# Scan layer on one core: the last time block's sum over half of the states moved from VectorE to GpSimd, and a new order around it

## The chip, the core and the metric

The kernel runs on 1 core of one Trainium2 chip, in float32. The metric is the device time of one execution in microseconds (us). Engines are named as the profile does: PE is TensorE, PEld its weight loads, DVE VectorE, ACT ScalarE, POOL GpSimd, SP SyncE.

## The reference

Two sequences (B = 2) of 1024 steps and 256 features pass a row filter, a selective state-space layer with 16 states over 512 channels, and then a much smaller attention and feed-forward part whose result is one row per sequence. The changed work is in the state-space layer:

```python
xi = jax.nn.silu(conv(xi) + conv_b)          # 4 taps over time, per channel
dt, Bm, Cm = split(xi @ x_proj)
delta = jax.nn.softplus(dt @ dt_w + dt_b)
def step(h, inputs):
    d_t, x_t, B_t, C_t = inputs
    dA = jnp.exp(d_t[..., None] * A)
    h = dA * h + (d_t * x_t)[..., None] * B_t[:, None, :]
    y = jnp.einsum('bds,bs->bd', h, C_t)     # sum over the 16 states
    return (h, y)
y = (y + xi * D) * jax.nn.silu(z)
return x + y @ out_proj
```

## The kernel before

The 2 x 1024 steps are cut into four chunks of T = 512 steps (`NCH` = 4, two per sequence, `c` = 0 to 3). In a chunk the 16 states (`NS`, `s`) are worked one after another; `n = 16 * c + s` counts them over the whole loop, 0 to 63. The 512 channels are 4 tiles `m` of 128 partitions, and the 512 steps are 4 time blocks `i` of 128. For one state the work goes round the engines:

- GpSimd, `input_step(n, pair)`: delta * x * B for two tiles at a time into a slot of the ring `hb` of `RING` = 4 states (L1353). It may run four states ahead; a slot is free once the transposes of state n - 4 are done.
- ScalarE, `exp_step(n, m)`: the decay `dA` of one tile into one of two PSUM halves (L1217); the half is free once the scan two tiles back is done.
- VectorE, `scan_step(n, m)`: the scan over 512 steps of a tile (L1686).
- TensorE, `transposes(n, i)`: time block `i` of all four tiles, turned so that time lies on the partitions, into PSUM half `hT[i % 2]` (L794). Blocks 0 and 2 use half 0, blocks 1 and 3 half 1, and a half must have been read before it is written again.
- Blocks 0 and 2 are multiplied by C by ScalarE, `mul_step` (L1227, into `hc`), and summed over the states in PSUM by TensorE, `reduce`. Blocks 1 and 3 are multiplied and summed by VectorE in one instruction, `mac_step`, called the sum step here (L1702, into `yTd`).

The loops of the engines run one state behind each other: in the iteration of state n, VectorE scans state n and then sums state n - 1, and ScalarE and TensorE work on the transposes of n - 1. An iteration has two halves, h = 2n and 2n + 1: tiles 0, 1 with block 1's sum, and tiles 2, 3 with block 3's sum.

Beside this run jobs: what the next chunk needs (prologue) and what the last chunk leaves (epilogue). Their order is written by hand, as tables from half-iteration to jobs. T: transposed input; I: input projection of a tile; V: four convolution taps of a tile by TensorE (3 tiles; tile 1, `POOL_TILE`, is convolved by GpSimd in `conv_taps`, L1386 to L1391); X: projection to dt, B and C; XT: C transposed; D: delta of a tile; Z: gate of a tile; Y: the sums of blocks 1 and 3 turned back; O: output projection. TensorE makes a job in its half, after that half's transposes; ScalarE and VectorE read it one half later:

```python
def to_read(h):
    return BESIDE[h - 1] if h else []
```

V is read by ScalarE (half of it as a copy, then a tanh, L1024 and L1025) and then by VectorE (L1483). D is read by ScalarE (absolute value L1066, then exponential and logarithm L1086 and L1088, with a load of the function table before the first) and then by VectorE (L1497). Jobs alternate between two PSUM banks, so a job waits until the one two places back is read. GpSimd also makes a diagonal scaling for each chunk (`row_scaling`, L1372) and the products of delta and x for the next chunk (`step_times_input`, L1403).

## Time and profile before

| | us |
|---|---|
| three runs | 580.72, 580.25, 576.88 |
| median | 580.25 |
| profiled execution | 581.45 |
| its span from first to last instruction | 579.3 |
| busy PE, PEld | 481.0, 339.3 |
| busy DVE, ACT, POOL | 485.7, 352.5, 357.9 |
| scan loop, first scan to last | 43.6 to 512.3 |

All busy times and rows are of the one profiled execution. The scan loop is the part from 43.6 to 512.3 us; before it lies the head for the first chunk, after it the attention and feed-forward rows. An engine's busy time in the whole says little here, since the four chunks differ in what they carry.

### The profile page before, as it was taken

What the parts mean: (1) busy time and instruction counts of PE and PEld (TensorE: products, weight loads), DVE (VectorE), ACT (ScalarE), POOL (GpSimd) and SP (SyncE); (2) the same over time, 40 slices, a digit from 0 to 9 for tenths busy, and PEclk for the clock granted to TensorE, in tenths of its full rate; (3) what the DMA queues carried; (4) which work ended last, traced back from release to release, by engine and by line L of the source; (5) the groups of instructions that cost most, each with busy time, mean ns of one, the idle gap of its engine ahead of it and who ended that gap; (6) DMA issues with size and microseconds to landing.
All of it is one profiled execution on the core that took longest, in us unless ns stands there. A gap on an engine that the chain in (4) does not pass through costs nothing.

```text
span 579.3 us, 7844 instructions
## 1 busy us (share of the span) xinstructions
PE 481.0 (83%) x2753; PEld 339.3 (59%) x2753; DVE 485.7 (84%) x569; ACT 352.5 (61%) x612; POOL 357.9 (62%) x215
## 2 busy tenths in 40 slices
PE   8968998789668999796689998966897867889992
PEld 6424664465457666554566665545785555878651
DVE  4779989987999899989998999799999989861512
ACT  3765666678765667886757768877466557521210
POOL 5039699747884698777856987787567548100001
PEclk9979999857999999979999999799998879699997
DMA  9331011110111011111110110111111860019004
GB/s 292 101 112 36 37 37 37 39 38 36 37 36 37 36 39 40 36 37 37 38 36 26 48 40 37 37 37 36 38 37 37 294 259 1 1 47 369 13 1 150
DMA packets 17918, 38.87 MB, mean 67 GB/s; under 512 B 1665, under 2 KB 10497, under 8 KB 17874
## 3 DMA queue, kind: packets, MB, share of 16 engines
q1 hardware_dynamic: 17874, 38.32, 19.0%
q8 instruction: 24, 0.39, 0.3%
q14 instruction: 20, 0.16, 0.1%
HBM read 36.08 MB, written 2.23 MB: 66 GB/s over the span
## 4 chain that ended last, share of the span: by engine, by line
PE 36%; DVE 33%; issue 16%; ACT 7%; POOL 6%; DVEq 0%; POOLq 0%; ACTq 0%
DVE scanmem L1686 19%; DVE yTd L1702 8%; PE hT L794 6%; PE pp L508 5%; POOL scanmem L1353 5%; PE pp L532 4%; PE pp L592 3%; PE yacc L566 3%; PE dA L765 2%; PE pp L558 2%; ACT hc L1227 2%; DVE yTd L1611 1%; PE pp L736 1%; PE yacc L562 1%; PE pp L664 1%
## 5 line engine op out<-in xcount | busy, mean ns | idle before, releaser
L1353 POOL TENSOR_TENSOR scanmem<-par,scanmem 128x1024 f32<-128x1024 f32 x128 | 299.1, 2362 | 94.7 <-PE hT L794 59.8
L1217 ACT ACTIVATE dA<-par,Aneg 128x512 f32<-128x512 f32 x256 | 172.5, 690 | 71.3 <-DVE scanmem L1686 70.2
L794 PE MATMUL hT<-con,scanmem 128*128 128x128 f32 x1024 | 158.7, 293 | 60.5 <-DVE yTd L1702 36.8
L794 PEld LDWEIGHTS hT<-con,scanmem 128*128 128x128 f32 x1024 | 122.0, 149 | 118.7 <-DVE yTd L1702 49.0
L1686 DVE TENSOR_TENSOR_SCAN scanmem<-dA,carry,scanmem 128x512 f32<-128x512 f32 x128 | 156.9, 1269 | 2.5 <-ACT dA L1217 2.4
L1686 DVE TENSOR_TENSOR_SCAN scanmem<-dA,scanmem 128x512 f32<-128x512 f32 x128 | 149.2, 1208 | 3.4 <-ACT dA L1217 3.0
L1227 ACT ACTIVATE hc<-hT,CTs 128x512 f32<-128x512 f32 x128 | 87.2, 681 | 78.1 <-PE hT L794 77.6
L1702 DVE SCALAR_TENSOR_TENSOR yTd<-hT,CTs,yTd 128x512 f32<-128x512 f32 x120 | 87.9, 733 | 10.9 <-PE hT L794 10.7
L566 PE MATMUL yacc<-con,hc 128*128 128x128 f32 x512 | 77.1, 293 | 5.8 <-ACT hc L1227 5.8
L566 PEld LDWEIGHTS yacc<-con,hc 128*128 128x128 f32 x512 | 63.2, 151 | 10.0 <-ACT hc L1227 6.5
L508 PE MATMUL pp<-xnT,wi 128*128 128x512 f32 x120 | 63.1, 658 | 5.1 <-ACT xnT L993 3.2
L532 PE MATMUL pp<-xr,diag 128*128 128x512 f32 x88 | 39.4, 592 | 0.0
L508 PEld LDWEIGHTS pp<-xnT,wi 128*128 128x128 f32 x120 | 23.1, 212 | 25.4 <-issue 18.6
L1423 POOL TENSOR_TENSOR par<-xt,hc 128x1024 f32<-128x1024 f32 x1 | 2.4, 2352 | 52.8 <-ACT hc L1269 52.8
L592 PE MATMUL pp<-wo,par 128*128 128x256 f32 x128 | 28.9, 380 | 0.8 <-DVE par L1467 0.8
L592 PEld LDWEIGHTS pp<-wo,par 128*128 128x128 f32 x128 | 23.8, 191 | 4.0 <-DVE par L1467 1.1
L532 PEld LDWEIGHTS pp<-xr,diag 128*128 128x128 f32 x88 | 16.0, 190 | 16.8 <-issue 16.5
L558 PE MATMUL pp<-dbc,wdt 17*128 17x512 f32 x28 | 19.8, 807 | 2.8 <-DVE par L1497 2.8
L1497 DVE SCALAR_TENSOR_TENSOR par<-pp,par 128x512 f32<-128x512 f32 x14 | 9.6, 690 | 13.2 <-ACT par L1088 10.5
L765 PE MATMUL dA<-con 128*128 128x128 f32 x110 | 17.1, 289 | 0.0
L765 PEld LDWEIGHTS dA<-con 128*128 128x128 f32 x110 | 13.9, 192 | 4.7 <-issue 4.6
L1386 POOL TENSOR_SCALAR par<-xr,half_w,half_b 128x512 f32<-128x512 f32 x3 | 2.3, 762 | 23.0 <-ACT xr L1013 23.0
(194 smaller groups left out, 487.8 us busy)
## 6 DMA issues: line engine op xcount, KB each, us to landing
scanmem<-brow SPq DMA_DIRECT2D x32, 512.0 KB, 3.6
par<-in SPq DMA_DIRECT2D x1, 4096.0 KB, 18.1
scanmem<-in SPq DMA_DIRECT2D x1, 4096.0 KB, 15.1
xt<-in SPq DMA_DIRECT2D x4, 512.0 KB, 6.5
wi<-in SPq DMA_DIRECT2D x2, 1024.0 KB, 6.7
out<-par SPq DMA_DIRECT2D x4, 512.0 KB, 4.1
aw<-in SPq DMA_DIRECT2D x5, 256.0 KB, 6.6
xr<-in SPq DMA_DIRECT2D x1, 1024.0 KB, 8.8
```

The source lines that it names most:

```text
L508: last = mm(o, win[:, k, col:col + P], xnT[:, k, :], start=k == 0, stop=k == KD - 1)
L532: last = mm(o, dg[:, m, k, :], xr3[:, m, k:k + T], start=k == 0, stop=k == KC - 1)
L558: return mm(o, wdt[:, m * P:(m + 1) * P], dbc[0:DR + 1, :], start=True, stop=True)
L566: return mm(o[:, m * P:(m + 1) * P], src, ident, start=False, stop=last, is_transpose=True, skip_group_check=True)
L592: last = mm(o[:, i * DM:(i + 1) * DM], dx(e)[:, m, t0:t0 + P], wo[:, m, :], start=m == 0, stop=m == CT - 1)
L765: mm(dst, ident, ident, start=True, stop=True)
L794: last = nc.tensor.transpose(hT[:, i % 2, m * P:(m + 1) * P], hb[:, n % RING, m, i * P:(i + 1) * P], ident)
L1217: A(dA[:, m % 2, :], delta(c)[:, m, :], ACT.Exp, scale=Aneg[:, m * NS + s:m * NS + s + 1]).then_inc(da_ready, 1)
L1227: A(hc[:, e % 2, :], hT[:, 0, :], ACT.Copy, scale=CTs[:, c % 2, i, s:s + 1]).then_inc(mul_done, 1)
L1353: nc.gpsimd.tensor_tensor(hb[:, n % RING, ms, :], dx(c)[:, ms, :], Bb[:, row:row + 1, :].to_broadcast([P, 2, T]), ALU.mult).then_inc(bx_re ...
L1686: V.tensor_tensor_scan(hb[:, n % RING, m, :], dA[:, m % 2, :], hb[:, n % RING, m, :], start, ALU.mult, ALU.add).then_inc(scan_done, 1)
L1702: V.scalar_tensor_tensor(dst, src, cs, dst, ALU.mult, ALU.add).then_inc(mac_done, 1)
```

## The change

The sum over the states for block 3 of 38 of the 64 states is split: ScalarE multiplies the transposed block by C into SBUF (`pool_mul_step`) and GpSimd adds it to `yTd` (`add_step`). These are the odd states of chunks 0 to 2 and states 1 to 14 of chunk 3 (`by_pool`). In GpSimd's program the addition for state n - 4 stands between the two `input_step`s of state n. TensorE's transposes of block 1 of state n wait for ScalarE's product where state n - 1 is such a state. Then the order:

- ScalarE makes `exp_step(n + 1, 0)` ahead of the second part of the reading of a job (V's tanh, D's softplus), and that part in the first half behind `exp_step(n, 2)`.
- VectorE reads V and D (`LATE`) one half later than before, behind the half's first scan.
- I of tile 1 is made first, and GpSimd's taps lie at states 5, 6 and 7 where they were at 4 and 5; its finishing of the tile at 9 (7 before), the step times input at 14 and 15 (13 and 14 before).
- X moves from slot 14 to 15, O of the second half from 16 to 17, D and Z to one slot each, up to 26.

```diff
@@ -50,21 +50,23 @@
-PROLOGUE = {3: [("T", 0), ("T", 1)], 4: [("I", 0)], 5: [("I", 1)], 6: [("I", 2)], 7: [("I", 3)], 8: [("V", 0)],
-            10: [("V", 2)], 12: [("V", 3)], 14: [("X", 0)], 18: [("XT", 0), ("D", 0)], 20: [("D", 1), ("D", 2)], 21: [("D", 3)],
-            22: [("Z", 0)], 23: [("Z", 1)], 24: [("Z", 2)], 25: [("Z", 3)]}
-EPILOGUE = {1: [("Y", 1), ("Y", 3)], 11: [("O", 0)], 16: [("O", 1)], 28: [("R", 0)], 30: [("R", 1)]}
+PROLOGUE = {3: [("T", 0), ("T", 1)], 4: [("I", 1)], 5: [("I", 0)], 6: [("I", 2)], 7: [("I", 3)], 8: [("V", 0)],
+            10: [("V", 2)], 12: [("V", 3)], 15: [("X", 0)], 18: [("XT", 0), ("D", 0)], 20: [("D", 1)], 21: [("D", 2)], 22: [("D", 3)],
+            23: [("Z", 0)], 24: [("Z", 1)], 25: [("Z", 2)], 26: [("Z", 3)]}
+EPILOGUE = {1: [("Y", 1), ("Y", 3)], 11: [("O", 0)], 17: [("O", 1)], 28: [("R", 0)], 30: [("R", 1)]}
 LAST_EPILOGUE = {1: [("Y", 1)], 2: [("Y", 3)], 3: [("O", 0)], 5: [("O", 1)], 17: [("R", 0)], 19: [("R", 1)]}
 ATT = [6, 8, 8, 10, 12, 14, 15, 16, 17, 20, 22, 23, 24, 27]
 ATT1 = [28, 29]
 HEAD_CONV = 2
 EARLY_I = [2, 3, 0, 1]
 POOL_TILE = 1
-POOL_AT = [4, 5]
+FIRST_I = POOL_TILE
+POOL_AT = {5: range(0, 2), 6: range(2, 3), 7: range(3, KC)}
 SCALING_AT = 3
-DX_AT = [13, 14]
-POOL_TANH_AT = 11
-POOL_FINISH_AT = 7
+DX_AT = [14, 15]
+POOL_TANH_AT = 12
+POOL_FINISH_AT = 9
+LATE = ("V", "D")
 def product_convs(n):
...
@@ -141,9 +143,35 @@
 INDEX = {job: q for q, job in enumerate(ORDER)}
+def by_pool(n):
+
+    c, s = n // NS, n % NS
+    return 0 < s < NS - 1 if c == NCH - 1 else s % 2 == 1
+
+
+def pool_sums(n):
+
+    return sum(by_pool(j) for j in range(n + 1))
+
+
+def vector_sums(n, i):
+
+    return 2 * n + (i + 1) // 2 - pool_sums(n if i == 3 else n - 1)
+
+
 def to_read(h):
     return BESIDE[h - 1] if h else []
+
+
+def read_by_vector(h):
+
+    return [job for job in to_read(h) if job[0] not in LATE]
+
+
+def read_late(h):
+
+    return [job for job in to_read(h - 1) if job[0] in LATE] if h else []
...
@@ -248,6 +276,10 @@
         def gate(n):
             return par[n % 2][:, 3, :].rearrange("p (m t) -> p m t", m=CT)
+        def for_pool(n):
+            room = xnT if n // NS == NCH - 1 else sm[:, :].rearrange("p (a t) -> p a t", t=T)
+            return room[:, pool_sums(n) % 2, :]
+
         def scaling(n):
             return par[n % 2][:, 1, 0:NT * P].rearrange("p (i t) -> p i t", i=NT)
...
@@ -568,7 +601,10 @@
             def job_Y(job, o):
                 _, e, i = job
-                pe.wait_ge(mac_done, 2 * (NS * (e + 1) - 1) + i // 2 + 1)
+                n = NS * (e + 1) - 1
+                pe.wait_ge(mac_done, vector_sums(n, i))
+                if i == 3 and by_pool(n):
+                    pe.wait_ge(pool_sum_done, pool_sums(n))
                 if e < NCH - 1:
                     for m in range(CT):
                         skip(o, e, i, m, m == 0)
...
@@ -787,9 +823,15 @@
                 if i == 0:
                     pe.wait_ge(scan_done, CT * (n + 1))
                 e = 2 * n + i // 2
-                if e >= 1:
-
-                    pe.wait_ge(mac_done if i % 2 else mul_done, e)
+                if i % 2 == 0 and e >= 1:
+                    pe.wait_ge(mul_done, e)
+                if i == 3:
+                    pe.wait_ge(mac_done, vector_sums(n, 1))
+                if i == 1 and n:
+                    if by_pool(n - 1):
+                        pe.wait_ge(pool_mul_done, pool_sums(n - 1))
+                    else:
+                        pe.wait_ge(mac_done, vector_sums(n - 1, 3))
                 for m in range(CT):
                     last = nc.tensor.transpose(hT[:, i % 2, m * P:(m + 1) * P], hb[:, n % RING, m, i * P:(i + 1) * P], ident)
                 last.then_inc(hT_ready, 1)
...
@@ -1022,8 +1064,11 @@
                     act.wait_ge(half_ready, 1)
                 A(xi(n)[:, m, :], o, ACT.Identity, bias=half_b[:, m:m + 1], scale=0.5)
+                return None
+
+            def product_tanh(job, o):
+                m = job[2]
                 A(o, o, ACT.Tanh, bias=half_b[:, m:m + 1], scale=0.5).then_inc(product_tanh_ready, 1)
-                return None
             def ev_X(job, o):
...
@@ -1142,8 +1187,8 @@
                     exp_ln_table()
                 if name == "D":
                     softplus(n, i)
-                if name == "S1":
-                    softmax(n)
+                if name == "V":
+                    product_tanh(job, bank(job))
             def read(job):
                 if job[0] in evs:
...
@@ -1226,6 +1274,15 @@
                     act.wait_ge(red_done, e - 1)
                 A(hc[:, e % 2, :], hT[:, 0, :], ACT.Copy, scale=CTs[:, c % 2, i, s:s + 1]).then_inc(mul_done, 1)
+            def pool_mul_step(n):
+
+                c, s = n // NS, n % NS
+                if by_pool(n):
+                    act.wait_ge(hT_ready, NT * n + 4)
+                    if pool_sums(n) > 2:
+                        act.wait_ge(pool_sum_done, pool_sums(n) - 2)
+                    A(for_pool(n), hT[:, 1, :], ACT.Copy, scale=CTs[:, c % 2, 3, s:s + 1]).then_inc(pool_mul_done, 1)
+
             def carry_step(n):
                 c, s = n // NS, n % NS
                 if c % HALVES == 0:
...
@@ -1235,21 +1292,30 @@
             for c in range(NCH):
                 for s in range(NS):
                     n = c * NS + s
-                    exp_step(n, 0)
+                    if n == 0:
+                        exp_step(n, 0)
                     exp_step(n, 1)
                     if n:
                         mul_step(n - 1, 0)
                     for job in to_read(2 * n):
                         read(job)
+                    exp_step(n, 2)
+                    for job in to_read(2 * n):
+                        after_job(job)
                     if c + 1 < NCH and 2 * s == POOL_TANH_AT:
                         pool_conv_tanh(c + 1)
-                    exp_step(n, 2)
                     exp_step(n, 3)
                     if n:
                         mul_step(n - 1, 2)
-                        carry_step(n - 1)
                     for job in to_read(2 * n + 1):
                         read(job)
+                    if n + 1 < NCH * NS:
+                        exp_step(n + 1, 0)
+                    for job in to_read(2 * n + 1):
+                        after_job(job)
+                    if n:
+                        pool_mul_step(n - 1)
+                        carry_step(n - 1)
                     if c + 1 < NCH and 2 * s + 1 == POOL_TANH_AT:
                         pool_conv_tanh(c + 1)
             n = NCH * NS
...
@@ -1354,6 +1420,18 @@
             own = Own(pool, pool_own)
+            def add_step(n):
+
+                c = n // NS
+                if by_pool(n):
+                    if by_pool(n - 1):
+                        pool.wait_ge(pool_sum_done, pool_sums(n - 1))
+                    else:
+                        pool.wait_ge(mac_done, vector_sums(n - 1, 3))
+                    pool.wait_ge(pool_mul_done, pool_sums(n))
+                    dst = yTd[:, c % 2, 1, :]
+                    nc.gpsimd.tensor_tensor(dst, dst, for_pool(n), ALU.add).then_inc(pool_sum_done, 1)
+
             def conv_finish(n):
                 acc, t = xi(n)[:, POOL_TILE, :], delta(n)[:, POOL_TILE, :]
...
@@ -1408,14 +1486,18 @@
                     if c + 1 < NCH and s == SCALING_AT:
                         row_scaling(c + 1)
                     input_step(n, 0)
+                    if n >= RING:
+                        add_step(n - RING)
                     input_step(n, 1)
                     if c + 1 < NCH and s == POOL_FINISH_AT:
                         conv_finish(c + 1)
                     if c + 1 < NCH and s in DX_AT:
                         step_times_input(c + 1, (0, 1) if s == DX_AT[0] else (2, 3))
                     if c + 1 < NCH and s in POOL_AT:
-                        conv_taps(c + 1, range(0, 2) if s == POOL_AT[0] else range(2, KC))
-
+                        conv_taps(c + 1, POOL_AT[s])
+
+            for n in range(NCH * NS - RING, NCH * NS):
+                add_step(n)
             pool.wait_ge(hT_ready, NCH * NS * NT)
             nc.gpsimd.memset(ff, 0.0).then_inc(ff_zero, 1)
             pool.wait_ge(row_copied, 1)
...
@@ -1688,7 +1770,8 @@
             def mac_step(n, i):
                 c, s = n // NS, n % NS
-                e = 2 * n + i // 2
+                if i == 3 and by_pool(n):
+                    return
                 dve.wait_ge(hT_ready, NT * n + i + 1)
                 dst = yTd[:, c % 2, i // 2, :]
                 src, cs = hT[:, 1, :], CTs[:, c % 2, i, s:s + 1]
...
@@ -1698,25 +1781,32 @@
                     V.tensor_scalar(dst, src, cs, None, ALU.mult).then_inc(mac_done, 1)
                 else:
-                    dve.wait_ge(mac_done, e - 1)
+                    if i == 3 and by_pool(n - 1):
+                        dve.wait_ge(pool_sum_done, pool_sums(n - 1))
+                    else:
+                        dve.wait_ge(mac_done, vector_sums(n - 1, i))
                     V.scalar_tensor_tensor(dst, src, cs, dst, ALU.mult, ALU.add).then_inc(mac_done, 1)
             for c in range(NCH):
                 for s in range(NS):
                     n = c * NS + s
                     scan_step(n, 0)
+                    for job in read_late(2 * n):
+                        read(job)
                     scan_step(n, 1)
                     if n:
                         mac_step(n - 1, 1)
-                    for job in to_read(2 * n):
+                    for job in read_by_vector(2 * n):
                         read(job)
                     scan_step(n, 2)
+                    for job in read_late(2 * n + 1):
+                        read(job)
                     scan_step(n, 3)
                     if n:
                         mac_step(n - 1, 3)
                     if s == 0 and c:
                         gate_even(c - 1)
-                    for job in to_read(2 * n + 1):
+                    for job in read_by_vector(2 * n + 1):
                         read(job)
                     if c == 0:
                         batch1_rows(s)
```

ScalarE, around the first V job of chunk 2 (state 4), before. `dA` is `exp_step`, `hc` is `mul_step`, `par1<-pp` and `pp<-pp` are V's copy and tanh:

```order
L1217 ACTIVATE dA<-par0,Aneg 128x512 [waits scan_done] x2
L1227 ACTIVATE hc<-hT,CTs 128x512 [waits red_done,hT_ready]
L1233 ACTIVATE carry<-scanmem 128x4 [waits scan_done]
L1024 ACTIVATE par1<-pp,half_b 128x512 [waits red_done,job_full]
L1025 ACTIVATE pp<-pp,half_b 128x512
L1217 ACTIVATE dA<-par0,Aneg 128x512 [waits scan_done] x2
L1227 ACTIVATE hc<-hT,CTs 128x512 [waits red_done,hT_ready]
```

And in the change, where `sm<-hT` is the new product for GpSimd:

```order
L1265 ACTIVATE dA<-par0,Aneg 128x512 [waits scan_done] x2
L1275 ACTIVATE hc<-hT,CTs 128x512 [waits red_done,hT_ready]
L1066 ACTIVATE par1<-pp,half_b 128x512 [waits red_done,job_full]
L1265 ACTIVATE dA<-par0,Aneg 128x512 [waits scan_done]
L1071 ACTIVATE pp<-pp,half_b 128x512
L1284 ACTIVATE sm<-hT,CTs 128x512 [waits pool_sum_done,hT_ready]
L1290 ACTIVATE carry<-scanmem 128x4 [waits scan_done]
L1265 ACTIVATE dA<-par0,Aneg 128x512 [waits scan_done]
```

The two exponentials that stood behind the tanh are apart now: one stands before it, the other behind the new product and the carry.

GpSimd, at states 1 to 3 of chunk 2, before. `scanmem<-par0` is `input_step`, `par1<-con,scl` the row scaling:

```order
L1353 TENSOR_TENSOR scanmem<-par0,scanmem 128x1024 [waits hT_ready] x2
L1353 TENSOR_TENSOR scanmem<-par0,scanmem 128x1024 [waits hT_ready,bb_in2]
L1353 TENSOR_TENSOR scanmem<-par0,scanmem 128x1024 [waits hT_ready]
L1372 TENSOR_SCALAR par1<-con,scl 128x128 [waits scan_done,scl_ready]
L1372 TENSOR_SCALAR par1<-con,scl 128x128 x3
L1353 TENSOR_TENSOR scanmem<-par0,scanmem 128x1024 [waits hT_ready] x2
```

And in the change, from the second `input_step` of state 1 on, where `yTd<-yTd,sm` is the addition for state 15 of chunk 1:

```order
L1419 TENSOR_TENSOR scanmem<-par0,scanmem 128x1024 [waits hT_ready]
L1419 TENSOR_TENSOR scanmem<-par0,scanmem 128x1024 [waits hT_ready,bb_in2]
L1419 TENSOR_TENSOR scanmem<-par0,scanmem 128x1024 [waits hT_ready]
L1450 TENSOR_SCALAR par1<-con,scl 128x128 [waits scan_done,scl_ready]
L1450 TENSOR_SCALAR par1<-con,scl 128x128 x3
L1419 TENSOR_TENSOR scanmem<-par0,scanmem 128x1024 [waits hT_ready]
L1433 TENSOR_TENSOR yTd<-yTd,sm 128x512 [waits pool_mul_done,mac_done]
L1419 TENSOR_TENSOR scanmem<-par0,scanmem 128x1024 [waits hT_ready]
```

The addition stands behind the row scaling and the first `input_step` of state 3.

TensorE, first state of chunk 2, before: the two Y jobs (`diagD`, then `yTd`) and the first transposes behind them:

```order
L562 MATMUL pp<-par1,diagD 128x128 [waits mac_done,job_free1]
L562 MATMUL pp<-par1,diagD 128x128 x3
L566 MATMUL pp<-con,yTd 128x128 x4
L562 MATMUL pp<-par1,diagD 128x128 [waits mac_done,job_free0]
L562 MATMUL pp<-par1,diagD 128x128 x3
L566 MATMUL pp<-con,yTd 128x128 x4
L794 MATMUL hT<-con,scanmem 128x128 [waits mul_done,scan_done]
L794 MATMUL hT<-con,scanmem 128x128 x3
L794 MATMUL hT<-con,scanmem 128x128 [waits mac_done]
```

And in the change:

```order
L595 MATMUL pp<-par1,diagD 128x128 [waits mac_done,job_free1]
L595 MATMUL pp<-par1,diagD 128x128 x3
L599 MATMUL pp<-con,yTd 128x128 x4
L595 MATMUL pp<-par1,diagD 128x128 [waits pool_sum_done,mac_done,job_free0]
L595 MATMUL pp<-par1,diagD 128x128 x3
L599 MATMUL pp<-con,yTd 128x128 x4
L836 MATMUL hT<-con,scanmem 128x128 [waits mul_done,scan_done]
L836 MATMUL hT<-con,scanmem 128x128 x3
L836 MATMUL hT<-con,scanmem 128x128 [waits pool_mul_done]
```

The order is the same; the second Y job now waits for GpSimd's addition as well, and the transposes of block 1 for ScalarE's product.

## Rows read from the trace of the kernel before

**Rows 1.** By stretch, the four chunks of the scan loop (start:end us, length, busy us of each engine)

```profile
43.60:167.30 123.70, 102.70 (x503) 66.88 (x501) 115.36 (x131) 85.07 (x149) 98.46 (x53) 0.89 0.11 39
167.30:284.20 116.90, 99.54 (x558) 69.60 (x556) 108.26 (x116) 82.77 (x134) 89.48 (x50) 0.96 0.11 37
284.20:399.30 115.10, 99.44 (x558) 69.56 (x556) 104.55 (x117) 83.86 (x148) 89.12 (x50) 0.96 0.11 38
399.30:512.30 113.00, 89.57 (x614) 74.06 (x613) 106.61 (x118) 65.70 (x109) 63.54 (x28) 0.89 0.23 86
```

**Rows 2.** Timeline of VectorE, quiet states of chunk 2 (start us, us)

```profile
387.11 0.73 DVE L1702 SCALAR_TENSOR_TENSOR yTd<-hT,CTs,yTd 128x512 f32<-128x512 f32 x1
387.75 2.33 DVE L1686 TENSOR_TENSOR_SCAN scanmem<-dA,scanmem 128x512 f32<-128x512 f32 x2
390.00 0.73 DVE L1702 SCALAR_TENSOR_TENSOR yTd<-hT,CTs,yTd 128x512 f32<-128x512 f32 x1
```

**Rows 3.** Waits of VectorE in the scan loop (us, times, longest)

```profile
DVE par L1497 <- ACT par L1088: 10.5, 10, 1.2
DVE yTd L1702 <- PE hT L794: 8.6, 14, 1.9
...
DVE scanmem L1686 <- POOL scanmem L1353: 0.3, 1, 0.3
```

**Rows 4.** By stretch, two parts of chunk 2

```profile
301.70:349.10 47.40, 47.30 (x246) 32.21 (x247) 41.94 (x46) 33.15 (x61) 37.29 (x22) 1.00 0.10 35
349.10:399.30 50.20, 38.76 (x204) 25.50 (x202) 45.70 (x52) 40.48 (x71) 38.50 (x19) 0.90 0.13 43
```

**Rows 5.** Timeline of TensorE, around V's first product in chunk 2

```profile
319.51 1.04 PE L794 MATMUL hT<-con,scanmem 128*128 128x128 f32 x8
320.39 3.60 PE L532 MATMUL pp<-xr,diag 128*128 128x512 f32 x8
```

**Rows 6.** Timeline of ScalarE around V's copy and tanh, same place

```profile
318.28 0.69 ACT L1227 ACTIVATE hc<-hT,CTs 128x512 f32<-128x512 f32 x1 [1.94 <-PE hT L794]
318.87 0.20 ACT L1233 ACTIVATE carry<-scanmem 128x4 f32<-128x4 f32 x1
318.96 0.68 ACT L1024 ACTIVATE par<-pp,half_b 128x512 f32<-128x512 f32 x1
319.53 0.66 ACT L1025 ACTIVATE pp<-pp,half_b 128x512 f32<-128x512 f32 x1
320.10 1.31 ACT L1217 ACTIVATE dA<-par,Aneg 128x512 f32<-128x512 f32 x2
```

**Rows 7.** GpSimd's tap additions, durations (line's instructions: min/median/max ns)

```profile
L1391 POOL TENSOR_TENSOR par<-par x9: 1267/1272/1277, 72.5 to 319.5; 128x512 f32<-128x512 f32 x9
```

**Rows 8.** Timeline of GpSimd at the start of chunk 2

```profile
286.78 1.42 POOL L1372 TENSOR_SCALAR par<-con,scl 128x128 f32<-128x128 f32 x4
288.15 4.70 POOL L1353 TENSOR_TENSOR scanmem<-par,scanmem 128x1024 f32<-128x1024 f32 x2
...
309.06 0.76 POOL L1386 TENSOR_SCALAR par<-xr,half_w,half_b 128x512 f32<-128x512 f32 x1 [9.30 <-ACT xr L1013]
```

**Rows 9.** Timeline of ScalarE around D's softplus, chunk 2

```profile
352.88 0.60 ACT L1066 ACTIVATE par<-pp 128x512 f32<-128x512 f32 x1
353.50 1.28 ACT L983 ACT_TABLE_LOAD   x1
...
355.99 1.28 ACT L1217 ACTIVATE dA<-par,Aneg 128x512 f32<-128x512 f32 x2
```

**Rows 10.** Timeline of TensorE at the start of chunk 2

```profile
290.20 1.13 PE L562 MATMUL pp<-par,diagD 128*128 128x128 f32 x8
...
291.61 1.04 PE L794 MATMUL hT<-con,scanmem 128*128 128x128 f32 x8
```

**Rows 11.** By stretch, two places of chunk 2 for the granted clock

```profile
360.00:370.20 10.20, 9.40 (x26) 5.61 (x26) 8.08 (x10) 8.86 (x16) 7.14 (x4) 0.50 0.17 52
387.70:393.50 5.80, 3.73 (x30) 3.00 (x28) 5.80 (x7) 4.57 (x9) 4.13 (x2) 1.00 0.01 3
```

10 lines of the change are left out of this document (7 added, 3 removed).

## The prediction

> **What bounds the kernel now.** I read the table by stretch first. The four chunks of the scan loop take 123.7, 116.9, 115.1 and 113.0 us, 468.7 of the span's 579.3, and VectorE is busy for 91 to 94% of each [rows 1]; what comes after has none of the moved work. The reader's first thought is then that each instruction taken from VectorE is time gained. Its price is read from starts: a sum step starts at 387.11 and the next scan at 387.75, so it costs 0.64 us, and two scans cost 2.25 (387.75 to 390.00) [rows 2]. A state without other work takes 2 x (2.25 + 0.64) = 5.8 us. In chunks 1 and 3 a scan that starts from a carry is about 0.06 longer, and such a state takes 6.0.
>
> The second look is at what VectorE waits for in the loop: 10.5 us for ScalarE's softplus before the reading of D, 8.6 for TensorE's transposes, 0.3 for GpSimd [rows 3], and some more for exponentials and for the tanh before the reading of V. The third look changes the picture. In chunk 2, from 301.70 to 349.10, TensorE is busy for 47.30 of 47.40 us at full clock, VectorE for 41.94; from 349.10 to 399.30 it is the other way round, 38.76 against 45.70 of 50.20 [rows 4]. In states 2 to 8 of the chunk the next chunk's products (I, V, X) and the last one's O stand between the transposes, and TensorE's rows follow one another without a gap [rows 5]. Chunk 1 has the same jobs in the same slots and nearly the same shares [rows 1]. So for 47 of the 115 us of chunks 1 and 2 a shorter VectorE gains nothing, and anything that holds TensorE costs its full length. Chunk 0 has no O and VectorE has a count beside the states up to 8, and chunk 3 has no products: they follow VectorE.
>
> **The sum steps.** 38 steps leave VectorE, 8 for each of chunks 0 to 2 and 14 for chunk 3, each for its state's last time block: 38 x 0.64 = 24.3 us is the ceiling. The sum of state n-1 runs in the iteration of state n. In their place ScalarE gets 38 products of 128x512 out of PSUM (0.59 from start to start, as the same step takes from 318.28 to 318.87 [rows 6]) and GpSimd 38 additions of 128x512 in SBUF, 1.27 us each by its taps' addition of the same shape [rows 7].
>
> GpSimd makes two products a state, 4.70 us for both [rows 8]. With an addition in every state of chunk 3 that is 5.9 against 5.4 for VectorE (6.0 less 0.64). Over the chunk its busy time goes from 63.54 [rows 1] by 14 x 1.27 to 81.3 us of about 105, and it runs up to four states ahead, so I cost it at nothing there; if its lead were gone it would bound the state at 5.9 and the gain would be 0.1 in place of 0.64.
>
> Chunk 3: the iterations of states 0, 4 to 7 and 10 to 13 have VectorE without waits, 9 x 0.64 = 5.8. In that of state 8 the sum also has a wait for a transpose in front of it; without both the next exponential is late next, and I take 1.0. State 9 gives 0.64, states 2 and 3, behind O, some 0.3 each; 14 and 15 wait for TensorE and give nothing. Sum 8.0. Chunk 0: iterations 2, 6 and 8 give 1.9 together.
>
> **The late readings.** V and D are now read behind the next half's first scan, and ScalarE's tanh or softplus is behind that scan's exponential. For D each wait of about 1.0 us gets a scan of 1.13 as cover. In the last seven states of a chunk the prize is 3.2 (D), 1.2 (Z, now one slot later, its table load beside a shorter half) and three sum steps, 1.9: 6.3 us. I take 1.6 off, because D1 to D3 now lie in one half each and ScalarE becomes the bound in the iteration of state 11: four exponentials at 0.61, two products at 0.59 and two D of 1.8 (352.88 to 355.99 less the table load of 1.28 [rows 9]) are 7.3 us, against 4.5 + 1.3 + 1.2 = 7.0 for VectorE. So 4.7 for chunks 1 and 2. In chunk 0 the readings of D move 0.8 less far: 3.9. V in chunk 0: the iteration of state 4 loses a tanh wait, a wait for the transpose and the sum step (2.1), and TensorE's late start, below, takes 0.7 back: 1.4. Chunk 0 is 1.9 + 1.4 + 3.9 = 7.2.
>
> **What the new order holds up.** A transposed last block stays in its PSUM half until its reader is done. That was VectorE right behind the transposes; it is now ScalarE's product behind V's copy, the next exponential and V's tanh. At 318 us of chunk 2 [rows 6]: the product for block 2 at 318.28, V's copy at 318.87, the exponential at 319.44, the tanh at 320.05, the new product from 320.62 to 321.30. TensorE's next transposes run from 319.51, their second four, into that half, from 319.95, and V's product follows at 320.39 [rows 5]. They now start at 321.3: TensorE stands 1.35 us in a stretch in which it has no slack. This comes with each V whose iteration follows an odd state, that of 4 and that of 6: 2.7 us a chunk. X goes from slot 14 to 15 and O from 16 to 17. There they stood between the transposes of blocks 1 and 2 and covered the time until VectorE had emptied the half; now nothing does, in two iterations, about 0.9 each, and X also needs GpSimd's finished tile. GpSimd finishes it in state 9, behind two products and an addition, and needs some 1.9 us itself. Together 1.9. The stretch is 4.6 us longer, in chunks 1 and 2.
>
> At the start of chunks 1 and 2 the job Y of block 3 waits for GpSimd's addition for state 15. It is queued behind row scaling (286.78 to 288.15) and the first product of state 3 [rows 8], and GpSimd comes there some 2 us later than before, because two more additions precede and the step times input comes one state later. The addition ends about 8.9 us after the chunk's start, at 292.5 in this trace's times. TensorE took Y at 290.20 and the transposes at 291.61 [rows 10]. Behind Y stand those transposes, and for them wait ScalarE's product and VectorE's first sum step. 2.3 us later, and with nothing from the removed sum step: 2.2 lost. In chunk 3, Y of block 3 stands one slot later, behind those transposes, and no scaling precedes: nothing.
>
> The taps cost nothing. Before, GpSimd stood until 309.06 for tile 1 of I [rows 8]; now it is made first and the taps lie a state later, with states 5 and 6 in front of them. VectorE waited for GpSimd only once in the loop, 0.3 us [rows 3].
>
> **Sum.** Chunk 0 +7.2, chunks 1 and 2 each -2.2 - 4.6 + 4.7 = -2.1, chunk 3 +8.0: 11.0 us. The profiled execution took 581.45 (span 579.3, 2.1 around it); 570.4. The median of the runs is 1.2 under it: **569 us**. Bounds: without any hold-up (below) 555; with the late readings worth nothing 589.
>
> **Rivals.**
> *TensorE is not as full as its rows.* Weight loads cover 32.21 of the 47.40 us [rows 4]. If the stretch can take in 1.35 us holds, chunks 1 and 2 gain 0.6 + 4.7 each: 10.6 + 7.2 + 8.0 = 25.8, which gives 554.5. For it speaks that ends of matmuls are modelled, against it that each group starts where the last one's pitch ends, for 47 us. The Trainium skill (Perfetto Trace Analysis, Identifying the Most-Contended Engine) speaks for this rival: matmul busy time is a poor measure of headroom, and the busy share of the weight loads should be used, here 68%. By that rule the stretch has room; by the rows' starts it has none.
>
> *Slower.* One mechanism, the held PSUM half. If it costs 4.6 in chunk 0 as well, and ScalarE, which also has to reach the product behind D's softplus, leaves of the last seven states only the sum steps (1.9), then chunk 0 is -2.7, chunks 1 and 2 -4.9 each, and chunk 3, where half of the products come late, +4: 8.5 us more, 589. It decides against the change once a chunk loses more than about 8 us. Against it: in chunk 0 VectorE's count leaves TensorE room.
>
> *The clock.* From 360.00 to 370.20 the granted clock is 0.50 (1.2 GHz), after TensorE had stood repeatedly behind D; in 387.70 to 393.50, with transposes and sums of the hidden state nearly alone, it is 1.00 [rows 11]. If the new holes bring another such stretch into the full part, TensorE's 10.2 us there cost 5.1 more; in both chunks 10.2: 579, no change. Nothing in the traced states 2 to 8 has fallen so far. The Trainium skill (TensorE: Matmul & The Clock Gate, Part 4: PE-mode transpose) says that transposes don't count as activity in the same way, which would favour this rival; the stretch from 387.70 does not bear it out.
>
> *GpSimd comes too late everywhere*, so that the even states' sum steps on VectorE wait for its additions as long as they save: 580. Its additions end 2 to 6 us before they are needed by my count, outside the chunk starts.
>
> **Chances.** Forecast 0.45 (own range 563 to 576); the full gain, 555, 0.25; clock or GpSimd, 580, 0.20; slower, 589, 0.10. A measurement of this kernel tells about 1% from no change, 574.4 to 586.1. Faster 0.68, same 0.22, slower 0.10. The range, 553 to 583, leaves out the slower case and the outer part of the best.
>
> **What would show it.** A hole of over 1 us before the second four transposes in the iterations of states 4 and 6 of chunks 1 and 2, ended by ScalarE's new product; Y waiting for GpSimd at the start of chunks 1 and 2; the waits before D's reading gone down from 10.5 to under 4; quiet states of chunk 3 at 5.4; chunk 1 and 2 about 2 us longer, chunk 0 and 3 each 7 to 8 shorter. It is wrong if chunks 1 and 2 shrink by 5, or if GpSimd's products stand in front of scans.

## The result, and the profile after

The changed kernel takes 592.53 us (median of 4 runs, 591.54 to 593.26), the kernel before 580.38 in the same comparison: a ratio of 1.0215, 95% interval 1.0174 to 1.0257. It is slower, by 1.7 to 2.6%. The forecast was 569, range 553 to 583. One run of e6 (1625.71 us) and one of e7 (644.65 us) in the experiments below were slow ones, and are left out of their medians.

From here on, and in the expectations of the experiments, "block 0" to "block 3" are what the prediction calls chunks 0 to 3 (the last one is also called the last time block); a quarter of a chunk is called a time block `i`.

The four blocks of the scan loop, by stretch, cut at the first scan of each block; they answer to [rows 1] (start:end us, length, busy us of PE, weight loads, DVE, ACT, POOL, granted clock, DMA share, GB/s):

```profile
44.33:164.35 120.02, 102.71 (x503) 67.38 (x501) 108.97 (x125) 87.82 (x156) 104.17 (x59) 0.89 0.10 36
164.35:292.88 128.53, 106.50 (x554) 76.78 (x553) 103.87 (x108) 85.91 (x142) 101.58 (x59) 0.88 0.10 35
292.88:418.23 125.35, 104.14 (x562) 74.29 (x560) 100.31 (x108) 87.31 (x156) 96.79 (x57) 0.92 0.10 33
418.23:524.40 106.17, 82.64 (x617) 69.59 (x616) 97.96 (x103) 73.09 (x124) 84.69 (x44) 0.95 0.26 96
```

VectorE's busy time fell in every block, as it should. Blocks 1 and 2 are 11.7 and 10.3 us longer all the same, and blocks 0 and 3 are 3.7 and 6.8 shorter. VectorE has less to do and waits longer. Its waits in the loop, which answer to [rows 3]:

```profile
DVE yTd L1788 <- PE hT L836: 25.4, 17, 4.3
DVE scanmem L1768 <- ACT dA L1265: 22.2, 30, 2.1
DVE yTd L1781 <- PE hT L836: 9.6, 3, 6.5
DVE par L1571 <- ACT par L1105: 4.7, 4, 1.5
DVE par L1579 <- ACT par L1133: 3.8, 4, 1.5
```

The wait for D's softplus (last row) went from 10.5 to 3.8 us, as forecast; the fourth row is the wait before the reading of Z. The waits for TensorE's transposes went from 8.6 to 35.0 (first and third row), those of the scans for an exponential from 5.4 to 22.2. In the following, the length of a state is the time from the start of its first scan to that of the next state's. Summed over thirds of a block it says where the time went (us, before and changed):

| | states 0-2 | states 3-8 | states 9-15 |
|---|---|---|---|
| block 0 | 24.5, 24.1 | 47.5, 46.1 | 51.7, 49.8 |
| block 1 | 22.4, 28.3 | 43.2, 46.6 | 51.3, 53.6 |
| block 2 | 22.1, 23.9 | 42.8, 48.0 | 50.2, 53.4 |
| block 3 | 22.5, 24.8 | 40.8, 36.2 | 49.7, 45.2 |

**The start of a block.** The timeline of GpSimd, TensorE and VectorE of the changed kernel, start of block 1 (start us, us):

```profile
170.11 1.43 POOL L1450 TENSOR_SCALAR par<-con,scl 128x128 f32<-128x128 f32 x4
171.50 2.35 POOL L1419 TENSOR_TENSOR scanmem<-par,scanmem 128x1024 f32<-128x1024 f32 x1
173.80 1.27 POOL L1433 TENSOR_TENSOR yTd<-yTd,sm 128x512 f32<-128x512 f32 x1
...
175.22 2.04 PE L595 MATMUL pp<-par,diagD 128*128 128x128 f32 x8 [4.86 <-POOL yTd L1433]
...
179.86 0.75 DVE L1781 TENSOR_SCALAR yTd<-hT,CTs 128x512 f32<-128x512 f32 x1 [6.51 <-PE hT L836]
```

GpSimd scales its rows, makes an input product and only then adds the last time block of state 15. TensorE stood 4.86 us for that addition, in front of Y, and then ran Y at the low clock (the eight products take 2.04 us, and 1.13 in [rows 10]). The transposes behind Y were late, and VectorE stood 6.51 us. In block 2 TensorE's hole was 2.69 us, in block 3 2.98.

**The late tile.** X of the next block reads all four tiles of the convolution, and GpSimd makes one of them. Its timeline and TensorE's in block 2:

```profile
352.94 2.36 POOL L1419 TENSOR_TENSOR scanmem<-par,scanmem 128x1024 f32<-128x1024 f32 x1
355.27 0.62 POOL L1439 TENSOR_SCALAR par<-par 128x512 f32<-128x512 f32 x1
355.97 1.26 POOL L1441 TENSOR_TENSOR par<-par 128x512 f32<-128x512 f32 x1
357.19 4.67 POOL L1419 TENSOR_TENSOR scanmem<-par,scanmem 128x1024 f32<-128x1024 f32 x2
...
357.29 2.78 PE L577 MATMUL pp<-par,wx 128*49 128x512 f32 x6 [1.78 <-POOL par L1441]
...
361.13 0.75 DVE L1788 SCALAR_TENSOR_TENSOR yTd<-hT,CTs,yTd 128x512 f32<-128x512 f32 x1 [4.27 <-PE hT L836]
```

X's last six matmuls wait 1.78 us for the tile that ends at 357.2, and behind X stand the transposes for which VectorE waits 4.27 us.

**The held half** came as the prediction drew it, at its price. ScalarE and TensorE of the changed kernel, as in [rows 5, 6] but in the iteration of state 4:

```profile
328.82 0.69 ACT L1275 ACTIVATE hc<-hT,CTs 128x512 f32<-128x512 f32 x1 [1.94 <-PE hT L836]
329.40 0.68 ACT L1066 ACTIVATE par<-pp,half_b 128x512 f32<-128x512 f32 x1
329.98 0.69 ACT L1265 ACTIVATE dA<-par,Aneg 128x512 f32<-128x512 f32 x1
330.59 0.66 ACT L1071 ACTIVATE pp<-pp,half_b 128x512 f32<-128x512 f32 x1
331.16 0.69 ACT L1284 ACTIVATE sm<-hT,CTs 128x512 f32<-128x512 f32 x1
...
331.91 0.66 PE L836 MATMUL hT<-con,scanmem 128*128 128x128 f32 x4 [1.25 <-ACT sm L1284]
```

The hole is 1.25 us, where 1.35 was forecast.

**State 11.** The same state by stretch, before, changed, and in the run with the order alone (e1 below, where this state ran at full clock). Before:

```profile
364.89:374.41 9.52, 9.52 (x38) 5.90 (x38) 7.25 (x9) 7.46 (x13) 5.58 (x5) 0.72 0.18 55
```

Changed:

```profile
381.88:391.37 9.49, 9.49 (x30) 5.82 (x29) 7.45 (x10) 7.44 (x15) 6.12 (x4) 0.50 0.05 22
```

Order alone:

```profile
373.94:380.91 6.97, 5.96 (x30) 3.30 (x29) 6.97 (x10) 6.43 (x13) 4.68 (x2) 1.00 0.11 30
```

At clock 1.00 VectorE is busy for all 6.97 us of this state, at 0.50 TensorE for all 9.49 us of it. The last seven states of blocks 0 to 2 had a mean granted clock of 0.80, 0.90 and 0.90 before and 0.79, 0.81 and 0.84 in the changed kernel.

### The profile page after: what moved, and what is told of

The parts are those of the page before. It is cut to its first block, busy times and chain, and to the rows that moved or that the text cites. A ratio compares the mean times of both kernels' runs of the same rounds, so it can differ in the third digit from the quotient of the medians.

```text
span 591.1 us, 7918 instructions
## 1 busy us (share of the span) xinstructions
PE 485.6 (82%) x2753; PEld 347.3 (59%) x2753; DVE 461.5 (78%) x531; ACT 369.3 (62%) x650; POOL 404.8 (68%) x253
## 4 chain that ended last, share of the span: by engine, by line
PE 50%; DVE 16%; issue 12%; ACT 11%; POOL 9%; DVEq 0%; ACTq 0%; POOLq 0%
PE hT L836 11%; DVE scanmem L1768 8%; PE pp L565 6%; PE pp L541 6%; POOL scanmem L1419 6%; PE yacc L599 5%; PE pp L628 4%; PE pp L591 3%; ACT dA L1265 2%; DVE yTd L1788 2%; PE pp L577 2%; PE dA L801 2%; POOL yTd L1433 2%; PE yacc L595 1%; ACT hc L1275 1%
## 5 line engine op out<-in xcount | busy, mean ns | idle before, releaser
L836 PEld LDWEIGHTS hT<-con,scanmem 128*128 128x128 f32 x1024 | 126.1, 152 | 105.6 <-issue 33.5
L599 PE MATMUL yacc<-con,hc 128*128 128x128 f32 x512 | 82.5, 304 | 11.6 <-ACT hc L1275 11.6
L1788 DVE SCALAR_TENSOR_TENSOR yTd<-hT,CTs,yTd 128x512 f32<-128x512 f32 x82 | 60.1, 733 | 28.1 <-PE hT L836 27.7
L599 PEld LDWEIGHTS yacc<-con,hc 128*128 128x128 f32 x512 | 67.6, 158 | 17.2 <-ACT hc L1275 13.5
L541 PE MATMUL pp<-xnT,wi 128*128 128x512 f32 x120 | 60.0, 629 | 4.9 <-ACT xnT L1035 3.2
L541 PEld LDWEIGHTS pp<-xnT,wi 128*128 128x128 f32 x120 | 22.1, 203 | 24.0 <-issue 17.7
L1433 POOL TENSOR_TENSOR yTd<-yTd,sm 128x512 f32<-128x512 f32 x24 | 30.6, 1276 | 1.2 <-ACT sm L1284 1.2
L1433 POOL TENSOR_TENSOR yTd<-yTd,xnT 128x512 f32<-128x512 f32 x14 | 17.8, 1270 | 12.7 <-ACT xnT L1284 12.7
L577 PE MATMUL pp<-par,wx 128*49 128x512 f32 x32 | 15.9, 625 | 2.8 <-POOL par L1441 2.4
L595 PE MATMUL pp<-par,diagD 128*128 128x128 f32 x64 | 9.4, 298 | 10.5 <-POOL yTd L1433 10.5
## 6 DMA issues: line engine op xcount, KB each, us to landing
par<-in SPq DMA_DIRECT2D x1, 4096.0 KB, 17.3
```

Source lines behind the costliest of these rows:

```text
L541: last = mm(o, win[:, k, col:col + P], xnT[:, k, :], start=k == 0, stop=k == KD - 1)
L599: return mm(o[:, m * P:(m + 1) * P], src, ident, start=False, stop=last, is_transpose=True, skip_group_check=True)
L836: last = nc.tensor.transpose(hT[:, i % 2, m * P:(m + 1) * P], hb[:, n % RING, m, i * P:(i + 1) * P], ident)
L1433: nc.gpsimd.tensor_tensor(dst, dst, for_pool(n), ALU.add).then_inc(pool_sum_done, 1)
L1788: V.scalar_tensor_tensor(dst, src, cs, dst, ALU.mult, ALU.add).then_inc(mac_done, 1)
```

## The experiments

Each kernel computes the whole reference, and each ratio is to the kernel before in the same comparison. "Old order" is the order of the kernel before in all tables and loops.

| kernel | order | states on GpSimd, blocks 0-2; block 3 | median us | ratio (95%) |
|---|---|---|---|---|
| changed | new | 1, 3, ... 15; 1-14 | 592.53 | 1.0215 (1.0174-1.0257) |
| e1 | new | none | 586.24 | 1.0116 (1.0042-1.0190) |
| e2 | old | 1, 3, ... 15; 1-14 | 581.79 | 1.0042 (1.0010-1.0074) |
| e3 | old | none; 1-14 | 568.27 | 0.9803 (0.9731-0.9876) |
| e4 | new | 1, 3, ... 13; 1-14 | 581.17 | 1.0020 (0.9985-1.0054) |
| e5 | old | as e4 | 577.17 | 0.9961 (0.9936-0.9987) |
| e6 | old, V and D read late | as e4 | 596.46 | 1.0282 (1.0227-1.0337) |
| e7 | old, early exponentials | as e4 | 582.72 | 1.0057 (1.0024-1.0090) |
| e8 | old, new slots | as e4 | 586.33 | 1.0100 (1.0039-1.0161) |
| e9 | old | 7, 9, 11, 13; 1-14 | 567.24 | 0.9774 (0.9740-0.9808) |
| e10 | old, state 1 added first | as e4 | 571.13 | 0.9846 (0.9793-0.9900) |
| e11 | new, finish in step 8 | as e4 | 574.62 | 0.9892 (0.9850-0.9934) |
| e12 | new, D read in place | as e4 | 582.44 | 1.0061 (1.0031-1.0091) |
| e13 | new, finish in step 8 | none | 587.49 | 1.0139 (1.0078-1.0200) |
| e14 | new, finish in step 8 | as changed | 585.81 | 1.0114 (1.0054-1.0175) |
| e15 | new, finish in step 8 | as e9 | 571.87 | 0.9887 (0.9829-0.9946) |
| e16 | old | 7, 9, 11-14; 1-14 | 562.08 | 0.9720 (0.9662-0.9778) |
| e17 | new, D and Z as before | none | 596.23 | 1.0275 (1.0196-1.0354) |
| e18 | new, X, D, Z as before | none | 587.56 | 1.0133 (1.0085-1.0181) |

### First set: order, move, and where (e1 to e4)

```diff
 def by_pool(n):
     c, s = n // NS, n % NS
-    return 0 < s < NS - 1 if c == NCH - 1 else s % 2 == 1
+    return False                                              # e1
+    return c == NCH - 1 and 0 < s < NS - 1                    # e3
+    return 0 < s < NS - 1 and (c == NCH - 1 or s % 2 == 1)    # e4
```

e2 and e3 also have the old tables, loops and LATE = (), with the new product behind the readings of its half state.

> The changed kernel in its new order, but no state is summed by GpSimd: VectorE sums all 64 as before. Theory M (the move costs, where the first three time blocks hand GpSimd half of their states): the order alone is near the kernel before, 575 to 582 us. Theory O (the new order of X, D, V, Z and of the exponentials costs, the move gains): 588 us or more. If both contribute, it lies between, and the part of the 12 us that is seen here is the order's.

> The order of the kernel before (tables, ScalarE's exponentials, VectorE's readings, GpSimd's taps), and the same 38 states summed by GpSimd. Theory M: as slow as the changed kernel or slower, 588 to 600 us. Theory O: 565 to 575 us, the gain that the prediction saw, and the order took it back.

> The kernel before, with the move in the last time block alone (states 1 to 14 of it), nothing else changed. The last block of the changed kernel was 6.8 us shorter. Theory M: that gain is the move's, and stands alone: 572 to 575 us. Theory O: in the last block the order's early exponentials made the gain, so the move alone is within 3 us of before, 577 to 583 us.

> The changed kernel, but the last state (15) of blocks 0 to 2 is summed by VectorE, so that the Y product at the start of the next block waits for no addition of GpSimd. Theory M with the Y wait as its main price: three holes of TensorE of 4.9, 2.7 and 2.9 us and what they push, 576 to 584 us. Rival, the holes move elsewhere since GpSimd is as late for the next work: 588 to 592 us.

Both parts of the change cost time by themselves, e1 6.0 us and e2 1.5, so neither theory holds as it stood: e1 lies between the two, e2 misses both. The third run turns the question round: the move in the last block alone gains 12.0 us, more than either theory said. In the traces 9.2 of it are block 3 (113.0 to 103.8). That this is 14 x 0.65 is chance: the iterations of states 2, 5, 6, 7, 11, 12 and 13 are 0.64 to 0.68 us shorter, as a sum step that leaves VectorE should make them, but those of 3, 9 and 10 together give nothing, and those of 8 and 14, where the clock was 0.81 and 0.50 and is now 1.00, give 1.8 and 2.6. State 14 before, and in e3:

```profile
498.41:506.48 8.07, 8.07 (x40) 8.07 (x41) 6.17 (x8) 3.63 (x9) 0.00 (x0) 0.50 0.00 0
488.53:493.97 5.44, 5.37 (x49) 4.49 (x49) 5.44 (x6) 4.67 (x9) 1.12 (x2) 1.00 0.00 0
```

At 0.50 TensorE bounded it, at 1.00 VectorE does; the order alone, with all sums on VectorE, has 6.02 us there. Another 3.3 us are in block 0, which e3 doesn't change (below). So about half of e3's gain came with a higher clock and not with the sum steps themselves, and why the clock is higher is not shown. The 24 states of the first three blocks cost 13.5 us in the old order (e2 against e3).

State 15 back on VectorE gave 11.4 us, as its theory said. State 1 of blocks 1 and 2 went from 13.8 and 9.5 to 7.2 and 7.0, states 1 and 2 of block 3 from 18.2 to 14.6. But block 2 did not get shorter (125.4): its state 8 grew from 10.3 to 11.9, with a wait for GpSimd's tile of 2.00 us (1.78) and a granted clock of 0.86 (1.00). Of the 11.7 us between the spans (591.1 and 579.4), 4.1 are in block 0 (120.0 to 116.0), whose program is the same in both up to its last state; there the mean clock of states 9 to 15 was 0.93, and 0.79 in the changed kernel. About a third of that difference is therefore the clock of block 0 and not the wait.

### Second set: the parts of the order, on 35 moved states (e5 to e8)

```diff
-LATE = ("V", "D")                        # e5, e7, e8: LATE = ()
+                    exp_step(n, 0)       # e5, e6, e8: exponentials in their old places,
+                    exp_step(n, 1)       # each function right behind its product's copy
-PROLOGUE = {... 15: [("X", 0)], ...}     # e5, e6, e7: old PROLOGUE, EPILOGUE,
-POOL_FINISH_AT = 9                       # POOL_AT, DX_AT, POOL_TANH_AT, POOL_FINISH_AT
```

> The order of the kernel before, and 35 states summed by GpSimd: states 1, 3, ..., 13 of blocks 0 to 2, states 1 to 14 of the last block. Against the move alone (581.8 us) only state 15 of three blocks is back on VectorE. Theory: the iterations with the Y product lose their 3.2 and 3.6 us of blocks 1 and 2, and nothing takes their place: 573 to 577 us. Rival (GpSimd is as late for the next product): 580 to 583 us.

> The kernel with the order of before and 35 states on GpSimd, and VectorE reads V and D behind the next scan (one of the three parts of the new order). The trace of the move alone shows VectorE waiting 1.1 to 2.0 us per state ahead of its readings of D in states 9 to 11. Theory: those waits fall, some 2 to 4 us below the same kernel with readings in place, 570 to 574 us. Rival: the bank of a product comes free one scan later, TensorE is held by as much, within 1.5 us of it or above.

> The kernel with the order of before and 35 states on GpSimd, with ScalarE's exponentials issued ahead of its products' functions (the second part of the new order). The move alone lost 3.1 us in state 3 of each of the first three blocks, with TensorE busy and ScalarE's product late. Theory: the early exponential takes that loss away, 3 x 3 us: 565 to 568 us. Rival: state 3's loss is the half of PSUM held for GpSimd's product, which the new order delays by one exponential more: 575 to 580 us.

> The kernel with the order of before and 35 states on GpSimd, with the new slots of I, X, D, Z and O and GpSimd's taps, finish and product of the step one or two states later (the third part of the new order). The order alone lost 3.6, 2.6 us in block 0 (states 8, 12), 1.7, 2.3 in block 1, 4.0, 1.4 in block 2. Theory: the slots did that, and it comes here too, 6 to 12 us above the same kernel with the old slots: 581 to 587 us. Rival: the exponentials or the late readings did it, and this is within 2 us of it.

e5 came as expected, at its upper edge. Of the three parts of the order, put on top of it one at a time, each costs: the late readings 19.3 us, the exponentials 5.6, the slots 9.2 (as e8's theory had it). All three together (e4) cost 4.0, so they are not independent prices.

The late readings were to gain, and lost most. With the old slots D1 and D2 share a slot, and the product of one half waits for the bank that the late reading still holds. TensorE of e6, block 2:

```profile
377.30 1.12 PE L591 MATMUL pp<-dbc,wdt 17*128 17x512 f32 x2
380.23 2.07 PE L591 MATMUL pp<-dbc,wdt 17*128 17x512 f32 x2 [1.81 <-DVE par L1574]
...
390.84 2.07 PE L591 MATMUL pp<-dbc,wdt 17*128 17x512 f32 x2 [4.94 <-DVE par L1574]
```

The second and third row wait for VectorE's late reading of D. States 10 and 11 take 10.6 and 12.4 us there, and 8.6 and 8.2 in e5.

In e5, e6 and e7 state 3 takes 9.4 to 11.3 us in each of the first three blocks, and 5.8 to 7.0 in e8. In e5's block 1 GpSimd's and VectorE's timelines name the cause:

```profile
189.36 0.77 POOL L1459 TENSOR_SCALAR par<-xr,half_w,half_b 128x512 f32<-128x512 f32 x1 [9.39 <-ACT xr L1055]
190.22 0.70 POOL L1462 TENSOR_SCALAR par<-xr,half_w 128x512 f32<-128x512 f32 x1
191.00 1.27 POOL L1464 TENSOR_TENSOR par<-par 128x512 f32<-128x512 f32 x1
192.23 2.35 POOL L1414 TENSOR_TENSOR scanmem<-par,scanmem 128x1024 f32<-128x1024 f32 x1
194.53 1.27 POOL L1428 TENSOR_TENSOR yTd<-yTd,sm 128x512 f32<-128x512 f32 x1
...
195.91 0.75 DVE L1783 SCALAR_TENSOR_TENSOR yTd<-hT,CTs,yTd 128x512 f32<-128x512 f32 x1 [3.34 <-POOL yTd L1428]
```

GpSimd stood 9.39 us for the input of its taps, had taps and an input product to make, and added state 1 behind them; VectorE's sum of state 2, an even state that was never moved, waited 3.34 us for it. So the theory of e7 was wrong, and its rival too: state 3 is GpSimd's, not ScalarE's.

### Third set: three repairs and a choice of states (e9 to e12)

```diff
+                    if n >= RING and s == 5:      # e10
+                        add_step(n - RING)
                     input_step(n, 0)
-POOL_FINISH_AT = 9
+POOL_FINISH_AT = 8                                # e11
-LATE = ("V", "D")
+LATE = ("V",)                                     # e12
```

e9 has the condition `s >= 7` for the odd states of blocks 0 to 2, in the old order.

> The order of before; GpSimd sums states 7, 9, 11, 13 of blocks 0 to 2 and states 1 to 14 of the last block (26 states). Against the last block alone (568.3 us) the trace of the 35-state kernel shows iterations 9 to 15 shorter by 1.2 to 1.9 us in each of blocks 1 and 2 and by some 0 to 4 in block 0. Theory (a state is worth moving where GpSimd has no other work between): 563 to 567 us. Rival (in blocks 0 to 2 any moved state only shifts the wait to TensorE): 567 to 571 us.

> The kernel with the order of before and 35 states on GpSimd (577.2 us), and in step 5 of each block GpSimd adds state 1 ahead of its first input product and not behind it. There the trace shows: taps 2.7 us, input product 2.35, then the addition, and VectorE's sum of state 2 waits 3.5 us for it. Theory: the addition comes 2.35 us earlier, the state is 2 us or more shorter in blocks 0 to 2: 569 to 572 us. Rival: the input product behind it is late instead, VectorE's scan waits: 575 to 579 us.

> The kernel with the whole new order and 35 states on GpSimd (581.2 us), and GpSimd finishes its tile of the convolution one state earlier (step 8, not 9). In its trace X waits for that tile 0.7, 0.6 and 2.0 us at state 8, and VectorE stalls 2.7, 2.3 and 6.6 us there. Theory: X waits no more, the states take about as long as before the change: 573 to 577 us. Rival: state 8's length is the bare TensorE work of X, moved into a stretch without cover, whatever GpSimd does: 579 to 583 us.

> The kernel with the whole new order and 35 states on GpSimd (581.2 us), but VectorE reads D in place again (V still behind the next scan). With the old slots the late readings cost 20 us, states 9 to 11 going from 24 to 31 us. Theory: the late reading of D costs in the new slots too, 3 or more us: 575 to 578 us. Rival: in the new slots, which give each part of D a place of its own, it costs nothing or gains: 580 to 585 us.

Moving one addition ahead of one input product gave 6.0 us (e10 against e5): states 3 to 8 are 1.8 and 3.6 us shorter in blocks 1 and 2 (and only 0.3 in block 0). State 3 went from 9.5 and 9.4 to 7.2 and 7.1; part of it came back in state 5 (7.5 and 7.1 to 9.8 and 9.7). VectorE's waits for additions stayed at 11.7 us in all (11.4 in e5): the wait behind the taps moved to a later addition, where less of it was lost. The size was as expected, the reason only in part. Finishing the tile one step earlier gave 6.6 (e11 against e4), as its theory said. In e11 the tile is done when X comes, 6.9 us ahead of it:

```profile
332.96 0.61 POOL L1439 TENSOR_SCALAR par<-par 128x512 f32<-128x512 f32 x1
333.66 1.27 POOL L1441 TENSOR_TENSOR par<-par 128x512 f32<-128x512 f32 x1
...
341.79 3.63 PE L577 MATMUL pp<-par,wx 128*49 128x512 f32 x8
```

e12's theory fell: in the new slots D's late reading is worth nothing either way (1.3 us, inside the spread), although VectorE waits 15.4 us before its readings of D in e12 and 3.4 in e4. In block 1 state 9 grew from 9.1 to 12.4 us and state 12 fell from 10.1 to 6.6. e9 is at the border of its two theories, 1.0 us below e3: the four late odd states gain little, in blocks 1 and 2 1.5 and 0.5 us.

### Fourth set: one price or two, the held half, and a rule (e13 to e16)

The edits are POOL_FINISH_AT = 8 on e1, on the changed kernel, and on e4 with `s >= 7`; for e16, on e9, the states are 7, 9, 11, 12, 13, 14.

> The new order alone (no state on GpSimd, 586.2 us), with GpSimd's finish of its tile one state earlier, in step 8. Theory: part of the order's own 6 us is this late tile (TensorE waited 1.3 us ahead of X in block 2, state 8 took 12.2, 7.7 and 9.3 us against 8.6, 6.8 and 6.6 before), and 2 to 4 us come back: 582 to 584 us; the rest is the late D and Z, which stay. Rival: without GpSimd's sums the tile is not late, within 1.5 us of 586.2.

> The changed kernel as it is (38 states on GpSimd, 592.5 us), with GpSimd's finish in step 8. Theory: the late tile and the Y product's wait are two prices that add up: here 6 us go as they did without state 15, 585 to 588 us. Rival: with state 15 moved, the wait at the start of a block gives GpSimd the time that the late tile needs, so that the tile was hardly late: 590 to 593 us.

> The whole new order, finish in step 8 and no state 15, and now without states 1, 3 and 5 of blocks 0 to 2 either: GpSimd sums 7, 9, 11, 13 and the last block's. Against the same kernel with them (574.6 us). The prediction priced the half of PSUM that a moved state holds at 1.3 us for states 3 and 5 each where TensorE is full, less 0.65 that VectorE saves. Theory: TensorE is the bound there and the moved states only cost: 3 to 6 us less, 569 to 572 us. Rival: VectorE's relief is worth as much as the hole, within 1.5 us of 574.6.

> The order of before; GpSimd sums states 7, 9, 11, 12, 13, 14 of blocks 0 to 2 and states 1 to 14 of the last block (32 states). States 13 and 15 have no product beside them and VectorE does not wait there (0.00 us of stall), so each sum of 0.65 us that leaves it is a gain: 2 x 0.65 x 3 = 3.9 us below the same kernel without states 12 and 14 (567.2 us): 562 to 565 us. Rival: GpSimd's product of the step stands there and the additions are late: 566 to 569 us.

The late tile and the late Y are two prices: the earlier finish gives 6.7 us with state 15 moved (e14) and 6.6 without. Without the sums it gives nothing in the time (e13). There was one wait of X to take away, of 1.33 us in block 2: its state 8 went from 9.3 to 7.7 us, but states 11 and 12 from 7.0 and 8.3 to 8.9 and 10.8, state 11 now at a clock of 0.50 where it was 1.00. So nearly all of the price of the late tile belongs to the move. Leaving states 1, 3 and 5 on VectorE gave 2.7 us (e15), at the edge of its theory (3 to 6). States 3 to 7, the ones with the held half, went from 37.9 to 36.4 us in block 1 and from 37.8 to 36.1 in block 2, and block 0's grew by 0.4. e16 met its theory's range: 5.2 us below e9, where 3.9 were worked out. Of the 3.9 the traces show 2.7 (states 12 to 15: 1.3, 0.4 and 1.0 us in blocks 0 to 2); state 8 of block 3, whose program is the same in both, is 1.5 shorter, and state 11 of block 2 1.6. VectorE in its block 2, states 13 and 14, four scans in a row with one sum between them:

```profile
376.20 4.55 DVE L1763 TENSOR_TENSOR_SCAN scanmem<-dA,scanmem 128x512 f32<-128x512 f32 x4
380.68 0.72 DVE L1783 SCALAR_TENSOR_TENSOR yTd<-hT,CTs,yTd 128x512 f32<-128x512 f32 x1
381.32 2.32 DVE L1763 TENSOR_TENSOR_SCAN scanmem<-dA,scanmem 128x512 f32<-128x512 f32 x2
```

States 13 and 15 take 5.73 and 5.44 us, and 6.38 and 5.78 in e9. e16 beats both kernels, by 2.8% (0.9720, 0.9662 to 0.9778) and by 30 us.

### Fifth set: what the order costs by itself (e17, e18)

```diff
-LATE = ("V", "D")
+LATE = ("V",)                                                   # both
-20: [("D", 1)], 21: [("D", 2)], 22: [("D", 3)], 23: [("Z", 0)], ...
+20: [("D", 1), ("D", 2)], 21: [("D", 3)], 22: [("Z", 0)], ...   # both
-15: [("X", 0)]
+14: [("X", 0)]               # e18, with the old POOL_AT, FINISH, TANH and DX_AT
```

> The new order alone (no state on GpSimd, 586.2 us), but D and Z in the slots of before, half a state earlier, and VectorE reads D in place. X stays half a state late, as do V's reading, the exponentials and GpSimd's work. Theory: what is left of the order's 6 us lies in states 9 to 15 of the blocks (54.1 and 50.8 us in blocks 1 and 2 against 51.3 and 50.2, state 12 alone 9.5 and 8.3 us against 7.2 and 7.0), so D and Z in place give back 3 to 5 us: 581 to 583 us. Rival: X half a state late leaves D in place without its transposed rows, and the wait only comes earlier: 585 us or more.

> The new order alone (no state on GpSimd, 586.2 us), with the whole chain of products from the input's convolution to Z as before: GpSimd's taps in steps 4 and 5 and its finish in 7, X, D and Z in the old slots, D read in place. What stays new is V's late reading, the exponentials ahead of the products' functions, the order of I and the second half of O one slot later. Theory: X's half state was the start of the order's price (with D and Z alone put back it took 596.2 us, D's matmuls waiting for X), so with X back too the order is as fast as before or a little faster: 576 to 581 us. Rival: the exponentials ahead of the functions, which cost 5.9 us on top of 35 moved states, cost here as well: 584 us or more.

Neither brought the kernel back to the time before; both theories fell, and both numbers are the rivals'. In e17 VectorE waits 17.3 us before its readings of D (3.4 in e1), and it is 10.0 us slower than e1. The rival of e18 named the exponentials, though, and e7 speaks against them: it shows no loss in states 8 and 9 (14.5 us in block 1, e5 14.2), though it has the same exponentials; e18 has 17.6 there. What e18 and e1 have and e7 hasn't is O's second half one slot later, right in front of the transposed rows of X and of D. TensorE of e18:

```profile
237.38 1.12 PE L591 MATMUL pp<-dbc,wdt 17*128 17x512 f32 x2 [1.25 <-DVE xt L1594]
```

D's first product waits for VectorE to read O out of the bank. That hole is in the changed kernel too (2.5 us in all). State 9 of e18 takes 11.6 and 11.7 us in blocks 1 and 2 and 8.2 in block 0, which has no O; before it took 7.7 in all three. That O's slot is the start of the order's 6 us is read from these traces; no kernel with O alone put back was run, so it is not shown.

## Why the prediction was wrong

The forecast was a gain of 11.0 us, the trace shows a loss of 11.8 (span 579.3 to 591.1). Below, a minus is time gained and a plus time lost. The steps, the one that failed most first:

**The late readings, the last seven states: -4.7 each in blocks 1 and 2 forecast, +2.4 and +3.2 measured.** This is the step that failed most, 15.0 us of the 22.8. It counted the waits before the readings as the prize, and the waits did go (10.5 to 3.8 us). But they were covered by others: the end of these states was set by TensorE and its banks, not by the order of VectorE's queue. e6 shows it at its worst (19.3 us lost), e12 shows the late reading of D to be worth nothing in the new slots: 12.0 us of waits came back and the time stayed. For state 11 the step named ScalarE as the new bound, with 7.3 us, and 7.0 for VectorE. At full clock VectorE bound it, with 6.97 (e1); in the changed kernel the state ran at 0.50 and TensorE bound it at 9.49. So up to 2.5 us of the miss in each block are the clock. State 12 has Z's table load now and takes 9.0 us in both blocks, before 7.2 and 7.0: what was a wait in state 11 stands in state 12. State 9 is 1.4 and 2.1 longer, behind O.

**The start of a block: +2.2 in blocks 1 and 2, nothing in block 3, forecast; +5.9, +1.8 and +2.3 measured (states 0 to 2).** The mechanism was right and its place too: Y waits for GpSimd's addition. In block 2 the size was right (the addition ended 8.4 us after the block's start; the forecast has 8.9, but its own time of 292.5 is 8.3 after 284.20; TensorE's hole 2.69, forecast 2.3). In block 1 the addition ended 10.7 us after the start, the clock fell during TensorE's hole, and the 2.3 became 6.5 for VectorE. For block 3 the prediction said that Y stands one slot later and is not late. It was late by 2.98 us: GpSimd worked almost without a break from 404.09 to 427.94, 9.7 us after the block's start, where before TensorE took this Y 6.7 us after it. The fall at the start of block 1 came with TensorE's hole there; busy for 4.99 us of 6.80, at 0.50:

```profile
173.40:180.20 6.80, 4.99 (x22) 4.69 (x23) 0.34 (x1) 1.20 (x2) 3.98 (x3) 0.50 0.21 76
```

**The clock.** This rival was right in part. In the full stretch the clock was 0.50 for 3.4 us in state 7 of each of blocks 0 to 2 (1.00 in all three before), in block 2 behind holes of TensorE of 1.25 and 0.63 us:

```profile
350.90:354.30 3.40, 2.89 (x15) 2.43 (x13) 3.40 (x5) 2.53 (x6) 3.40 (x3) 0.50 0.00 0
```

The longer falls were at the start of block 1 and in states 10 to 12. The Trainium skill (TensorE: Matmul & The Clock Gate, Part 4: PE-mode transpose) was cited beside this rival; no run here tells what transposes count for.

**The full stretch: +4.6 forecast, +3.4 and +5.3 measured (states 3 to 8).** Right in sum. The held half was right in size (1.25 us). X's wait for the tile was bundled with the moved slots at 1.9 us for both; e11 shows the tile alone at 6.6 us over three blocks. The prediction's first rival fell: the same states got longer although VectorE does less, and taking the moved states out made states 3 to 7 1.5 and 1.6 us shorter again (e15). By the rule beside it (the Trainium skill, Perfetto Trace Analysis, Identifying the Most-Contended Engine) the stretch had room, with weight loads busy for 68%; it had none for these holes.

**The sum steps.** Block 3: -8.0 forecast, -6.8 measured, with +2.3 of Y in it; with state 15 back it is -9.5 (e4), with the old order -9.2 (e3). The price of 0.64 us a state held where VectorE has no waits. That the sum is so near is luck: the forecast put state 14 at nothing, and it gave 2.7 us, with the clock at 1.00 where it had been 0.50. Block 0: -7.2 forecast, -3.7 measured; in e4, with the same program in all but its last state, it is -7.7, at a clock of 0.93 in its last seven states and not 0.79.

**The rivals.** Slower than before was given 0.10, by the held half alone. The bound of 589 that is given for late readings worth nothing is this rival's sum; its own terms (4.7 twice and 3.9) taken away make 582. The held half was not what decided: GpSimd came too late for its two readers on TensorE (Y 10.5 us of holes, X 2.4), and it was the rival "GpSimd too late everywhere" that had the right engine. It looked at VectorE's even sums only. In the new order these were never late; with the old order they were (3.34 us in state 3 of block 1 of e5). Of the signs named for the prediction the holes, the waits for Y, the waits before D's reading and the quiet states of 5.4 us in block 3 all came; the lengths of the blocks did not.

## What to carry to other kernels

Work that is moved to an engine with idle time arrives behind what stands in that engine's queue, so for each moved step ask who reads its result next and what is queued ahead of it there: here two readers on TensorE paid for GpSimd's 38 additions, and one step's place was worth 6 us. Move only steps whose iteration is bounded by the relieved engine without a wait (0.64 to 0.68 us came back in each of seven such iterations of block 3), and leave the others: 32 well chosen states gave 18 us, 38 with a new order around them cost 12. A wait in front of a reading is a prize only if nothing else, a bank or a full engine, is just as late behind it.

## What was not expected of the hardware

The same instructions ran at different clocks from one kernel to another. Block 0 of e3 is the program of the kernel before, and took 120.4 us against 123.7; up to its last state block 0 of e4 is that of the changed kernel, 116.0 against 120.0, with granted clocks of 0.93 and 0.79 in states 9 to 15. What differed ahead of it was the time to the loop's start (45.19 and 44.33 us); why the clock fell otherwise is not settled. By these two pairs (3.3 and 4.1 us), single effects of up to some 4 us can't be told from one trace of this kernel. The clock of e16's blocks 1 to 3 (0.94, 0.97, 0.97) is higher than the changed kernel's (0.88, 0.92, 0.95):

```profile
164.30:277.63 113.33, 99.62 (x556) 72.29 (x556) 104.63 (x111) 85.37 (x139) 97.58 (x57) 0.94 0.12 38
277.63:389.31 111.68, 97.58 (x558) 70.04 (x559) 100.95 (x110) 86.64 (x154) 95.70 (x56) 0.97 0.11 39
389.31:493.05 103.74, 80.81 (x619) 67.99 (x619) 98.70 (x103) 73.52 (x123) 83.28 (x43) 0.97 0.26 98
```
